# Second attention with the value matmul turned round: probabilities streamed through four column groups, row sums inverted as 16 columns and widened

## The reference

```python
def _attend(q, k, v, k_mask=None):
    scale = 1.0 / jnp.sqrt(jnp.asarray(HEAD_DIM, q.dtype))
    scores = jnp.einsum('bqnd,bknd->bnqk', q, k) * scale
    probs = jax.nn.softmax(scores, axis=-1)
    return jnp.einsum('bnqk,bknd->bqnd', probs, v)
...
q = rms_norm(x @ Wq + bq, gq).reshape(b, -1, n, d)              # 16 heads of 16
k_img = rms_norm(ctx_img @ Wk_img + bk_img, gk_img).reshape(b, -1, n, d)
v_img = (ctx_img @ Wv_img + bv_img).reshape(b, -1, n, d)
out = (txt_x + img_x).reshape(b, -1, n * d)
return out @ Wo + bo
```

## Time and profile before

| | |
|---|---|
| median of 3 runs | 911.52 us (909.61 to 912.76) |
| profiled execution, its own time | 911.44 us |
| span of the profiled execution | 909.7 us |
| mean granted TensorE clock | 0.902 |
| first scores of the second attention | 402.72 us |
| scores of its last tile | 490.28 us |
| last logit of the router | 517.1 us |

### The profile page before, as it was taken

One profiled execution on the slowest core, in us unless ns is written; L12 is line 12 of the kernel. 1 busy time (PEld: TensorE's weight loads), 2 busy tenths in 40 slices (PEclk: granted clock), 3 DMA queues, 4 the chain that ended last, 5 costly groups with the idle time before them and its releaser, 6 DMA issues.

```text
span 909.7 us, 12595 instructions
## 1 busy us (share of the span) xinstructions
PE 811.3 (89%) x3950; PEld 626.5 (69%) x3951; DVE 392.2 (43%) x1072; ACT 224.7 (25%) x399; POOL 200.8 (22%) x195
## 2 busy tenths in 40 slices
PE   4848978999999999989999726999999999999995
PEld 4526766888888888777777724666666666666663
DVE  5963775557656566516777372111111111111111
ACT  1412222111111111254555311222222222222221
POOL 3540180000000000151110043232232322323322
PEclk9755557999999999989999556999999999999999
DMA  9600000000000000294000610121211212112111
GB/s 210 248 0 0 1 1 0 1 1 1 1 1 0 0 0 0 90 429 174 1 0 0 225 59 24 24 35 23 35 28 30 35 23 35 29 29 35 23 28 17
DMA packets 23819, 43.10 MB, mean 47 GB/s; under 512 B 7825, under 2 KB 21138, under 8 KB 22386
## 3 DMA queue, kind: packets, MB, share of 16 engines
q1 hardware_dynamic: 16306, 32.55, 10.1%
q0 software_dynamic: 7488, 10.23, 6.8%
HBM read 33.20 MB, written 9.57 MB: 47 GB/s over the span
## 4 chain that ended last, share of the span: by engine, by line
PE 81%; DVE 10%; issue 2%; ACT 2%; DMA 2%; POOL 1%; SPq 0%; DVEq 0%; POOLq 0%; ACTq 0%
PE ps L1026 21%; PE ps L1045 12%; PE ps L798 8%; PE ps L799 8%; PE ps L800 8%; PE ps L926 3%; PE ps L1036 3%; PE ps L906 2%; ACT wexp L622 2%; PE ps L915 2%; PE ps L699 2%; PE ps L1015 2%; DVE t L1150 1%; PE ps L739 1%; PE ps L976 1%
## 5 line engine op out<-in xcount | busy, mean ns | idle before, releaser
L1026 PE MATMUL ps<-wexp,arena 128*128 x624 | 197.0, 469 | 0.6 <-ACT arena L667 0.6
L1026 PEld LDWEIGHTS ps<-wexp,arena 128*128 128x128 f32 x624 | 116.5, 192 | 66.0 <-issue 9.0
L1475 DVE TENSOR_TENSOR arena<-arena,ps 128x704 f32<-128x704 f32 x39 | 34.6, 888 | 244.2 <-ACT arena L674 244.2
L1045 PE MATMUL ps<-wexp,arena 128*128 x468 | 115.1, 387 | 1.0 <-ACT arena L682 1.0
L503 POOL DMA_INDIRECT out_rows<-arena,slot_row x39 | 61.8, 1585 | 231.3 <-DVE arena L1468 231.3
L1045 PEld LDWEIGHTS ps<-wexp,arena 128*128 128x128 f32 x468 | 85.5, 189 | 30.3 <-issue 14.2
L405 POOL TENSOR_TENSOR rstd<-ve,mhalf 128x2 f32 (+1 forms) x32 | 22.9, 714 | 346.8 <-DVE ve L1084 346.8
L798 PE MATMUL ps<-xn_high,gu_high 128*128 (+3 forms) x208 | 92.8, 446 | 0.2
L799 PE MATMUL ps<-xn_low,gu_high 128*128 (+3 forms) x208 | 82.7, 398 | 0.0
L800 PE MATMUL ps<-xn_high,gu_low 128*128 (+3 forms) x208 | 82.5, 397 | 0.0
L581 ACT ACTIVATE wexp<-ps 128x512 f32<-128x512 f32 (+1 forms) x52 | 31.0, 597 | 188.5 <-PE ps L800 188.5
(11 more groups left out here) (235 smaller groups left out, 1213.4 us busy)
## 6 DMA issues: line engine op xcount, KB each, us to landing
wexp<-in_wexp SPq DMA_DIRECT2D x8, 2176.0 KB, 22.2
wexp<-in_gu SPq DMA_DIRECT2D x2, 1632.0 KB, 9.4
out_rows<-x_sb SPq DMA_DIRECT2D x1, 2048.0 KB, 15.1
xn_rows<-xmem SPq DMA_DIRECT2D x4, 512.0 KB, 2.9
wexp<-in_dn SPq DMA_DIRECT2D x1, 1664.0 KB, 15.9
x_sb<-in_x SPq DMA_DIRECT2D x1, 1536.0 KB, 8.2
wexp<-in_ctxT SPq DMA_DIRECT2D x4, 256.0 KB
arena<-xn_rows,slot_row POOLq DMA_INDIRECT x39, 2.8
```

What stands on the lines that cost most here:

```text
L1026: mm = pe.matmul(bank(2 * part + half)[:, 0:HALF1], xt1[:, k % 2, h, :], wexp[:, bass.ds(expert + col, HALF1)], start=(h == 0), stop=(h == ...
L1045: mm = pe.matmul(bank(6)[:, 0:D], hT[0:n, c, :], wexp[0:n, bass.ds(expert + (KD * W13 + c * D), D)], start=(c == 0), stop=(c == C1 - 1))
L1475: dve.tensor_tensor(h1.rearrange("p (a n) -> p a n", a=2), sg1.rearrange("p (a n) -> p a n", a=2), bank(2, 2).rearrange("p (a n) -> p a n" ...
```

## The change

The second attention turns the value matmul round. The values (32 columns: two heads, no ones) are now the stationary operand, and the 128 columns of transposed probabilities are streamed past them; four such products go into the four groups of 32 array columns and so into PSUM partitions 0-31, 32-63, 64-95 and 96-127. The result comes out already transposed. The row sums come from a second set of eight such products, with a 0/1 selector `ssel`, into 128 more columns of the bank. ScalarE copies values and sums out (`copy_sums`), TensorE turns the sums back (`turn_sums`), VectorE inverts 16 columns (`invert_sums`), ScalarE widens them 16-fold (`widen_recs`), TensorE turns the two widened pieces (`spread_recs`), and VectorE multiplies (`divide`), writing `attT` for `project`, which now runs three tiles behind instead of two. The pipeline is written out over 19 steps instead of a loop, and all eight `route1` come after it.

```diff
-        vbd = sb("vbd", [P, B, H // 2, 2 * (HD + 1)])
+        vbd = sb("vbd", [P, B, H // 2, 2 * HD])
+        ssel = sb("ssel", [P, KD, 2 * HD])
...
+            def copy_sums(t):
+                act.wait_ge(c_pv, t + 1)
+                if t:
+                    act.wait_ge(c_sumT, t)
+                    act.wait_ge(c_att, t)
+                act.activation(wexp[:, last + 1024:last + 1408], bank(4)[:, 0:D + P], ACT.Copy).then_inc(c_sums, 1)
+
+            def widen_recs(t):
+                act.wait_ge(c_rec, t + 1)
+                if t:
+                    act.wait_ge(c_spread, t)
+                act.activation(recE.rearrange("p m (j r n) -> p m (j r) n", j=4, r=2),
+                               rec1[:, :].rearrange("p (m a) -> p m a", m=KD).unsqueeze(3).broadcast_to([P, KD, 8, HD]),
+                               ACT.Copy).then_inc(c_recE, 1)
...
                 if k:
+                    pe.wait_ge(c_sums, t)
+                if k == 0:
+                    pe.wait_ge(sel_done, 3)
+                for m in range(KD):
+                    for j in range(4):
+                        c = j // 2 * 4 + m * 2 + j % 2
+                        pe.matmul(bank(4)[32 * j:32 * j + 32, m * P:(m + 1) * P], vbd[:, b, m * 4 + j, :],
+                                  pT[:, k % 2, c, :], start=True, stop=True)
+                for m in range(KD):
+                    for j in range(4):
+                        c = j // 2 * 4 + m * 2 + j % 2
+                        mm = pe.matmul(bank(4)[32 * j:32 * j + 32, D:D + P], ssel[:, m, :], pT[:, k % 2, c, :],
+                                       start=(m == 0), stop=(m == KD - 1))
+                mm.then_inc(c_pv, 1)
+
+            def turn_sums(t):
+                pe.wait_ge(c_sums, t + 1)
+                if t:
                     pe.wait_ge(c_att, t)
-                for c in range(8):
-                    half, m, j = c // 4, c // 2 % 2, c % 2
-                    pair = m * 4 + half * 2 + j
-                    mm = pe.matmul(bank(4)[:, pair * 34:(pair + 1) * 34], pT[:, k % 2, c, :], vbd[:, b, pair, :],
-                                   start=True, stop=True)
-                mm.then_inc(c_pv, 1)
...
-                dve.tensor_copy(o[:, :, :, HD], half.broadcast_to([P, 8, 2])).then_inc(v_ready, 1)
...
+            def invert_sums(t):
+
+                dve.wait_ge(c_sumT, t + 1)
+                dve.reciprocal(rec1[:, :].rearrange("p (m j r) -> p j m r", m=KD, j=4),
+                               bank(5)[:, D:D + P].rearrange("p (j c) -> p j c", j=4)[:, :, 0:4].rearrange(
+                                   "p j (m r) -> p j m r", m=KD)).then_inc(c_rec, 1)
+
+            def divide(t):
+
+                dve.wait_ge(c_spread, t + 1)
+                if t:
+                    dve.wait_ge(c_proj, t)
+                dve.tensor_tensor(attT, attU, bank(5)[:, 0:D], ALU.mult).then_inc(c_att, 1)
```

More of the change, by code:

```diff
@@ L160, in program @@
         qt = view(arena, 3072, 2, KD, P)
-        att = view(arena, 3584, D)
-        attT = view(arena, 3840, KD, P)
+        attT = view(arena, 3584, KD * P)
+        attU = view(wexp, last + 1024, KD * P)
+        sumT = view(wexp, last + 1280, P)
+        recE = view(wexp, last + 1408, KD, P)
         filler = view(arena, 1024, D)
@@ L623, in copy_probs @@
                                ACT.Copy).then_inc(c_pT, 1)
-            def copy_att(t, k):
-                act.wait_ge(c_attT, t + 1)
-                act.activation(attT, bank(5)[:, 0:D].rearrange("p (k n) -> p k n", k=KD), ACT.Copy).then_inc(c_attTc, 1)
-            act.wait_ge(c_qT, B * KD)
[L631 to L638, removed]
@@ L639, in _ @@
-            pick_tile(0, 0)
[L640 to L655, removed]
+            def copy_sums(t):
[11 more added lines that the diff above has]
+                               ACT.Copy).then_inc(c_recE, 1)
@@ new lines, in _ @@
+            act.wait_ge(c_qT, B * KD)
+            pick_tile(0, 0)
+            for t in range(NT + 3):
+                if 2 <= t < NT + 2:
+                    copy_sums(t - 2)
+                if 2 <= t < NT + 2:
+                    widen_recs(t - 2)
+                if 1 <= t <= NT:
+                    copy_probs(t - 1, t - 1)
+                if t + 1 < NT:
+                    pick_tile(t + 1, t + 1)
+                if t < NT:
+                    exp_scores(t, t)
+                if t >= 6 and t % 2 == 0:
+                    copy_batch(3, t // 2 - 3, 0)
@@ L942, in project @@
                 for m in range(KD):
-                    mm = pe.matmul(bank(6)[:, 0:D], attT[:, m, :], wo1[:, m, :], start=(m == 0), stop=(m == KD - 1))
+                    mm = pe.matmul(bank(6)[:, 0:D], attT[:, m * P:(m + 1) * P], wo1[:, m, :], start=(m == 0), stop=(m == KD - 1))
                 mm.then_inc(c_proj, 1)
[L946 to L970, removed]
+            for t in range(NT + 3):
+                if t < NT:
+                    scores(t, t)
+                if 2 <= t < NT + 2:
+                    turn_sums(t - 2)
+                if 1 <= t <= NT:
+                    turn_probs(t - 1, t - 1)
+                if 2 <= t < NT + 2:
+                    spread_recs(t - 2)
+                if t >= 3:
+                    project(t - 3, t - 3)
+                if 1 <= t <= NT:
+                    values(t - 1, t - 1, (t - 1) // TB)
+                if t >= 6 and t % 2 == 0:
+                    turn_rows(3, t // 2 - 3, (t // 2 - 3) % 2)
             def route1(b):
@@ L980, in _ @@
             pe.wait_ge(c_shift, NT)
[L981 to L987, removed]
+            for b in range(4):
+                route1(b)
             turn_rows(3, B - 1, 1)
@@ L1321, in add_att @@
                 dve.tensor_tensor(x_sb[:, t, :], x_sb[:, t, :], bank(6)[:, 0:D], ALU.add).then_inc(x_new, 1)
[L1323 to L1347 removed]
+            for t in range(NT + 3):
+                if 2 <= t < NT + 2:
+                    invert_sums(t - 2)
+                if t < NT:
+                    maxima(t)
+                if 2 <= t < NT + 2:
+                    divide(t - 2)
+                if t < NT:
+                    centre(t)
+                if t == 3:
+                    dve.wait_ge(c_biased, B)
+                if t >= 3:
+                    add_att(t - 3, t - 3)
+                if t >= 4 and t % 2 == 0:
+                    dve.wait_ge(x_new, t - 3 + XB + 1)
+                    stats(3, t // 2 - 2)
+                if t >= 5 and t % 2:
+                    rows_of(3, (t - 5) // 2, (t - 5) // 2 % 2)
             rows_of(3, B - 1, 1)
```

77 lines of the change are left out of this document (26 added, 51 removed).

## The result

| | before | changed kernel |
|---|---|---|
| median, 20 runs each | 912.58 us (909.61 to 915.72) | 915.56 us (912.25 to 920.0) |
| ratio, 95% interval | | 1.0034 (1.0021 to 1.0047) |
| profiled execution | 911.44 us | 918.65 us |
| first scores to last logit, that execution | 114.4 us | 120.1 us |

The change makes the kernel slower by 0.34%, 3.0 us. The forecast was 920, so the sign was right and the size was not: +8.4 forecast, +3.0 measured. The forecast started from the first three runs of the kernel before (911.5); over twenty the median is 912.6, and from there the same +8.4 gives 921.

The account below looks back on a forecast made before the run. Today TensorE's order plus one exposed copy bounds the step; after the change, a loop through all engines. 911.44 - 1.3 (start) + 1.9 (12 steps) + 7.8 (drain) = 919.8, so 920 us; own range 915 to 925, wider range 909 to 932.

Parts of the forecast that it names:

- the loop through all engines: Attention steps: exponential, sums copied, turned, inverted, widened, `project`, `divide`, subtraction; 5.66 us, or 6.16 with `copy_batch`; +1.9 over 12 steps.
- the drain: From `scores(15)` to the last logit: 34.6 us after against 26.8 before, at the lower clock; +7.8.
- the term of 6.64 for `route1(0..3)`: In the drain, behind the last projection: 32 router passes priced at 6.64 us, as before at the lower clock.
- The start: The two steps before the 12 counted: sums' loop not yet closed, TensorE's shorter chain rules, 2 x 0.67 = -1.3 us.
- the dip of the clock: Within the 12 attention steps: one dip worth 1.66 us in the kernel before, assumed to stay as before.
- One sign: Attention chain: the copy, reciprocal and widening of the sums were to appear in it, with ScalarE's exponential.
- The value stage (1.3): TensorE's `values` in each step: 32 passes in 1.3 us, bounds 0.9 and 3.5, against 1.97 before.
- The rival in which the column groups do not overlap (941): Value stage: `values` takes 3.5 us, steps 6.85 or 7.1, +30, total 941 us; chance 0.12.
- the main case (34.6): Drain at the lower clock throughout: last logit 34.6 us after `scores(15)`.
- the rival with the higher clock (25.0): Drain stays at the higher clock, route work costs half, last logit at 25.0 us; total 910; chance 0.12.
- The rival in which the clock falls more often in attention: Attention steps: TensorE, less busy, gets the lower clock in four more steps; total 926 to 930 us; chance 0.13.
- The rival on the other side (908): Attention steps: TensorE's chain stays the bound, steps 4.65 or 4.9 us, total about 908 us; chance 0.08.

Follow-up runs that it names:

- the two edits that open it: On the changed kernel: subtraction of `centre` ahead of `divide`, 900.63 us (ratio 0.9885); or two `attT` buffers, 900.13 us (0.9887).
- its two edits: On the kernel before: `route1(0)` and `route1(1)` moved behind the last projection, 913.03 us (1.0013); or attention loops written out, 910.65 us (0.9982).
- With the loop open: Changed kernel with the subtraction of `centre` placed ahead of `divide` on VectorE: 900.63 us, ratio 0.9885, 12 steps in 57.6 us.

## Why the prediction was right in sign and wrong in size

In short: the loop through all engines was right, with its path and its price. What failed in size is the drain, forecast at +7.8 us and measured at +4.2, and within it the term of 6.64 for `route1(0..3)`, which took 3.9 to 4.4. The start and the dip of the clock were smaller misses of the same sign. That the median 915.56 lies inside the forecast's own range of 915 to 925 is luck in part: the sum started from a base that was 1.1 us low.

**The loop (+1.9 for 12 steps): right.** 70.3 and 70.4 measured, 69.9 forecast. Single terms, forecast and then measured in the chain and the timeline of the changed kernel's first profile: end of the subtraction to the end of `copy_sums` 1.57 and 1.56, with `copy_batch` 2.07 and 2.04; transpose of the sums done 0.38 and 0.37 later; invert and widen up to `spread_recs` 0.79 and 0.80; the two transposes ahead of `project` 0.28 and 0.27. The step is 5.71 for 5.66 and 6.20 for 6.16, and the steady steps of both profiles agree to 0.01 us. One sign was not met: the chain does not name the reciprocal and the widening, since `turn_probs` beside them fills that time to within 0.17 us. That this loop and no other held the time is shown by the two edits that open it and by the tripled value products, which change nothing. The last link, the subtraction "which now stands behind `divide` on VectorE", is worth 15 us, and so is the wait of `divide` for `project`: taking out either one opens the loop.

**The value stage (1.3): 1.0.** Off by 0.3, and without effect on the steady steps while the loop stands. The rival in which the column groups do not overlap (941) is refuted: 1.0 us, where it needed 3.5. The rule of the Trainium skill, "TensorE: Matmul & The Clock Gate", part 3, that a weight load overlaps a running matmul only when the row groups differ, does not by itself describe these rows: 16 weight loads of 32 columns take 0.38 us beside 16 passes in 0.65, all in the same rows. The same part also has loads pulled ahead that go to the background weight buffer, and that these rows do not contradict.

**The start (-1.3): too small.** The changed kernel measured 17.0 and 14.4 (14.5 with the groups reordered), mean 15.3; before 17.9, 19.2 and 17.7, mean 18.3: -3.0. I took 0.67 for each of two steps, the saving at the higher clock, as if the start ran there. It does not. The third step, from the scores of tile 2 to those of tile 3, in the kernel before, then in the changed kernel's first and second profile:

```profile
413.61:420.62 7.01, 6.76 (x39) 5.46 (x38) 3.55 (x5) 2.75 (x4) 0.00 (x0) 0.76 0.70 300
```

```profile
415.20:420.89 5.69, 4.79 (x56) 3.54 (x52) 2.85 (x4) 2.52 (x5) 0.00 (x0) 0.76 0.75 318
```

```profile
412.50:416.90 4.40, 3.65 (x56) 2.68 (x52) 2.79 (x4) 2.54 (x6) 0.00 (x0) 1.00 1.02 435
```

At the same mean clock of 0.76 the change saves 1.3 us in this step, twice the 0.67, and where the clock is 1.00 another 1.3. The clock does not rise earlier in the changed kernel: it rises 7 to 8.5 us behind the first scores in four of the five profiles with the old attention (three of the kernel before, one of each of its two edits) and in seven of the nine with the new one, and later in the others. But with the old attention it falls again within the third step in those four profiles, and with the new one it stays up in all nine. Why it stays was not tried and is open.

**The drain (+7.8): the step that failed.** Measured 32.8 and 31.2 (31.3 with the groups reordered), mean 31.8, against 26.8, 27.9 and 28.2 of before, mean 27.6: +4.2. Of the 3.6 us between +7.8 and +4.2, 0.8 is the base, since the one profile read for the forecast has the shortest drain of the three. The other 2.8 lie behind the last projection. The forecast said that "everything that was partly hidden stands in a row, at the prices of before at that clock", with `route1(0..3)` at 6.64 and 15.2 from there to the last logit; that took 12.0, 12.4 and 12.4. The first 32 passes took 3.87, 4.39 and 4.40, and the second 32 6.64 as forecast. So "I take the lower clock" is the choice that went wrong: it holds for half of the passes. In the first profile the granted clock was 0.50 ahead of the first 32 and rose after they had begun, to a mean of 0.91 in them (windows in the result section). In the second it was 1.00 ahead of them and fell in their course, to a mean of 0.77:

```profile
501.58:506.58 5.00, 3.17 (x18) 2.41 (x18) 2.06 (x6) 0.42 (x1) 0.35 (x1) 1.00 0.00 0
506.58:510.97 4.39, 4.39 (x34) 4.39 (x33) 2.07 (x12) 0.60 (x1) 0.70 (x1) 0.77 0.79 274
```

So the clock just ahead of the passes does not tell their price, and what makes it rise and fall there stays open. Both the main case (34.6) and the rival with the higher clock (25.0) missed a drain that is part one and part the other.

The way of the last tile, `scores(15)` to the end of `project(15)`, was forecast at 17.3 or 19.4 by clock; it took 20.8 and 18.8 (18.9 reordered), against 15.2 to 16.5 before. Of the +4.2 some 3.5 are this way (19.5 in the mean of three profiles against 16.0), and hardly the order of the router, as the kernel before with its router last indicates (26.6). The mean of 19.5 beside the forecast 19.4 is luck in part: in the second profile both projections ran at 1.00 (0.88 and 1.10), the case priced at 17.3, and the way still took 18.8, because the clock was down earlier, when TensorE turned the last probabilities (1.62 instead of 0.87).

**The dip (kept as before): gone.** Worth 1 us on average over the three profiles of before. (The forecast's 1.66 sets 7.12 against a 5.46 added up from rows; the steps between scores give 1.6.) The rival in which the clock falls more often in attention is refuted: 1.00 in both windows, and no step of the 12 is longer than the loop makes it, though TensorE is busy 9.3 us of 11.5 where it was busy 10.9 with 0.87.

**The sum.** Start -3.0, steps +2.3 against undisturbed ones, dips -1.0, drain +4.2: +2.5, for 3.0 between the medians. The profiles are too few to divide the half microsecond left. The forecast's +1.9, -1.3, +7.8 differ from that by 0.4, -1.7 and -3.6, and -1.0 for the dip.

**The rival on the other side (908).** It named the point rightly: TensorE's chain at 4.65, or 4.9 over two steps. With the loop open the mean is 4.80 (57.6 / 12), and the kernel takes 900.6. Its condition was wrong: no engine was quicker than I reckoned, the order of two calls closed the loop. Its drain was 6 to 7 us too long besides (27.6 measured with the loop open).

## What to carry to other kernels

Before a stage of the bounding engine is shortened, follow the chain from one step's instruction to the same instruction of the next through the other engines, with what stands ahead of each in its queue and each single buffer; if that loop is about as long as today's step, nothing is gained until it is opened, and here a second buffer or another order of two calls was worth 15 us, five times what the change itself moved. Price a start and a drain at both levels of the clock and take the two as bounds, not by the one busy row that is nearest: the same 32 passes cost 3.6 to 4.4 us or 6.64. Where effects of 3 us are to be told apart, read two or three profiles of each kernel, since start and drain alone vary by 1.3 to 2.6 us from one execution to the next.

## What the runs showed of the hardware

- A pass with a stationary operand of 32 columns and 128 moving ones took 0.03 us (0.57 and 0.44 for 16 in the chain), against 0.11 for 128 columns; and the order of the column groups made no difference.
- 32 router passes of 8 moving columns took 3.63 to 4.40 us where the mean granted clock in them was 0.97 to 0.76, and 6.64 at 0.50, with TensorE busy all the time in both. The clock just ahead did not decide: before the 3.63, 3.70 and 3.87 it stood at 0.50, before the 4.39 and 4.40 at 1.00.
- Less work on TensorE did not lower its clock: in attention it was busy 81% of the time at a granted 1.00 in the changed kernel, and 95% in a window of the kernel before with a dip to 0.87. The dip came in the same step in all three profiles that have it, and in two of five it did not come.
- The handoff from ScalarE's copy to TensorE took 0.14 to 0.16 us in three of four steps of the loop body and 0.04 in straight-line code.
